# Filter stage with the edge attributes in both halves of the partitions, and register loads without bounds instructions

## The chip, the cores and the metric

The kernel runs on one core of a Trainium2 chip. The metric is the device time of one execution in microseconds (us), median of the runs. One launch computes the whole reference.

## The reference

Four graph layers on 3125 nodes with 256 features and 50000 edges sorted by destination, each followed by a residual and a layer norm:

```python
x = _layernorm(x + _L0_gnn_ref(x, edge_weight, src, dst), axis=-1)      # a product of Givens rotations
x = _layernorm(x + _L1_gnn_ref(x, ..., edge_index, edge_type_2, ...))   # three relational attention layers
x = _layernorm(x + _L2_gnn_ref(x, edge_index, edge_weight, edge_attr_50, ...))
x = _layernorm(x + _L3_gnn_ref(x, edge_index, L3_gnn_W, L3_gnn_b))      # mean over the edges by source
```

The core of L2, which the filter stage computes, is

```python
Wf = ssp(ssp(edge_attr @ m1_W + m1_b) @ m2_W + m2_b)     # ssp(x) = softplus(x) - log 2; edge_attr is (50000, 50)
msg = h1[src] * (Wf * C[:, None])
agg = jax.ops.segment_sum(msg, dst, num_segments=n_nodes)
```

In L0, the list of rotations is packed into chunks in order of the edges; in L3, `h[col]` is gathered and summed per `row`, then divided by the degree.

## The kernel before

`build` writes the stages one after the other, each in a block with a barrier of all engines at its end. Three of them are touched.

**Listing** (`layer0_list`, 0 to 222 us of the trace). The rotations are handled in five batches of 25 partition rows. `make(b)` lets VectorE write one-hot tiles (`picked`, `valued`), TensorE multiplies them (L358), 13 rows and then 12, the two halves of a batch, and `gather(b)` adds each row's block of 32 columns from PSUM into `acc` at an offset that is read from SBUF into a register (L284 to L294). VectorE's order is make(0), make(1), gather(0), make(2), gather(1), and so on to make(4), gather(3), gather(4). gather waits for the half on the semaphore `packed`. The call at L284 loads the 13 or 12 offsets of a half with one register load and then runs bounds instructions on each.

**Filter** (`filter_sum`, 4240 to 5037 us). Edges are handled in tiles of 125, four tiles (HF = 4) a quad, 106 quads. P is 125 and D is 256. Per quad:
- SyncE (`load`) waits until the hidden product of two quads before is done, reads the four tile numbers from `etile` one by one (L2515) and issues four loads of 50 x 125 attributes into `ea` (L2516). Row 50 of `ea` stays 1.0 for the bias. `load_hots` brings the one-hot matrix `sel` that sums edges into nodes (L2522).
- GpSimd gathers the source rows `gx`, one indirect DMA a tile (L2499), four quads deep; it waits for `ms_made` of the quad whose buffer it reuses.
- TensorE runs a lap of three pieces in this order: `hidden` of quad n+4 (L2545: for o in 0, 1 the product of the weights' columns o and the attributes, 51 x 128 by 51 x 500, into two PSUM banks), `sums` of quad n (L2568, or L2573 for a quad that touches more than one node tile), `filters` of quad n+3 (L2556).
- ScalarE computes the softplus parts of hidden and filters in one round (L2593 abs, L2596 exp, L2599 log); it waits for `f2_made` and `hid`.
- VectorE runs make_f2 (L2632), make_h1 (L2626), products (L2638, L2641) and the adds into `agg` (L2646: one for a quad of one node tile, else four).

The order of the work is written out by hand: each engine has its own lap of four quads, and semaphores tie them together. All matrices are fp32; the compiled program has two weight loads and two matmul instructions (passes) for each product.

**Source** (`source_mean`, 5170 to 5902 us). GpSimd gathers 424 tiles of edges (L2970) into a ring of four halves of four tiles, TensorE sums each (L2982), VectorE adds the sums into `agg` at a tile number read into a register (L3004, L3009) and makes the one-hot matrix of a later half (L2999).

## Time and profile before

| | us |
|---|---|
| median of 3 runs (lowest, highest) | 5916.76 (5911.26, 5916.9) |
| the profiled execution's own time | 5903.53 |
| its span in the trace | 5901.7 |

| engine | busy us | share |
|---|---|---|
| TensorE matmul | 4003.0 | 68% |
| TensorE weight load | 2943.7 | 50% |
| VectorE | 3007.7 | 51% |
| ScalarE | 1975.2 | 33% |
| GpSimd | 3630.7 | 62% |

The shares are means over stages with different limits. Times in the trace are counted from the start of the span. An engine's idle time is put down to what ended it; "issue" means that the engine waited for nothing that the profile shows, so its own sequencer was at work or between instructions. A matmul's recorded duration is longer than the distance to the next, since they are pipelined.

### The profile page before, as it was taken

What the parts mean: (1) busy time and instruction counts of PE and PEld (TensorE: products, weight loads), DVE (VectorE), ACT (ScalarE), POOL (GpSimd) and SP (SyncE); (2) the same over time, 40 slices, a digit from 0 to 9 for tenths busy, and PEclk for the clock granted to TensorE, in tenths of its full rate; (3) what the DMA queues carried; (4) which work ended last, traced back from release to release, by engine and by line L of the source; (5) the groups of instructions that cost most, each with busy time, mean ns of one, the idle gap of its engine ahead of it and who ended that gap; (6) DMA issues with size and microseconds to landing.
All of it is one profiled execution on the core that took longest, in us unless ns stands there. A gap on an engine that the chain in (4) does not pass through costs nothing. (4 is left out here: it accounts for less than half of the span.)

```text
span 5901.7 us, 73554 instructions
## 1 busy us (share of the span) xinstructions
PE 4003.0 (68%) x17113; PEld 2943.7 (50%) x17121; DVE 3007.7 (51%) x6900; ACT 1975.2 (33%) x4675; POOL 3630.7 (62%) x2851
## 2 busy tenths in 40 slices
PE   5599932398577778777777534445599999645553
PEld 5488831254455554355555433333376777433332
DVE  6576636621455552255555434445367777533334
ACT  0022210010466661166565112221188888200000
POOL 0144422067787754587773788885677777478884
PEclk9999975599788888888887755556799999855655
DMA  0000001333666643466663333333344444243332
GB/s 8 23 11 11 11 14 39 95 81 67 166 176 170 165 113 99 111 176 170 166 165 90 68 80 85 82 85 82 81 120 120 119 119 119 72 103 83 84 83 72
DMA packets 510802, 558.08 MB, mean 95 GB/s; under 512 B 302100, under 2 KB 394239, under 8 KB 510285
## 3 DMA queue, kind: packets, MB, share of 16 engines
q0 software_dynamic: 349600, 362.07, 25.6%
q1 hardware_dynamic: 157688, 186.99, 11.1%
q10 hardware_dynamic: 3250, 6.40, 0.4%
q14 instruction: 208, 1.70, 0.1%
q8 instruction: 56, 0.92, 0.1%
HBM read 460.15 MB, written 92.22 MB: 94 GB/s over the span
## 5 line engine op out<-in xcount | busy, mean ns | idle before, releaser
L1261 POOL DMA_INDIRECT sum_gx_sb<-scratch_xw,keep_k_row_step_sb x1272 | 1588.1, 1248 | 425.2 <-issue 358.6
L1374 PE MATMUL sum_a_ps<-sum_gx_sb,sum_sel_sb 125*125 125x258 f32 (+1 forms) x4320 | 1189.8, 438 | 454.2 <-ACT sum_gx_sb L1310 178.3
L1374 PEld LDWEIGHTS sum_a_ps<-sum_gx_sb,sum_sel_sb 125*125 125x125 f32 x4320 | 917.4, 238 | 641.5 <-issue 451.5
L1310 ACT ACTIVATE sum_gx_sb<-sum_gx_sb,sum_wt_sb 125x129 f32<-125x129 f32 x3312 | 981.8, 388 | 539.0 <-DVE sum_wt_sb L1503 539.0
L2499 POOL DMA_INDIRECT filter_gx_sb<-scratch_h,keep_k_src_step_sb x424 | 603.3, 1423 | 174.3 <-issue 97.8
L1168 POOL DMA_INDIRECT scratch_grouped<-keep_k_value_sb,keep_k_place_sb x400 | 481.1, 1203 | 250.7 <-issue 133.8
L2970 POOL DMA_INDIRECT source_gx_sb<-scratch_h,source_grouped_sb x424 | 529.5, 1249 | 140.1 <-issue 115.7
L2982 PE MATMUL source_s_ps<-source_gx_sb,source_sel_sb 125*125 125x257 f32 x848 | 376.1, 621 | 306.3 <-DMA source_gx_sb<-scratch_h,source_grouped_sb 304.8
L2982 PEld LDWEIGHTS source_s_ps<-source_gx_sb,source_sel_sb 125*125 125x125 f32 x848 | 249.0, 307 | 433.4 <-issue 170.2
L2556 PE MATMUL filter_ps<-filter_m_sb,filter_h_sb 128*125 128x256 f32 x1696 | 385.4, 380 | 1.7 <-DVE filter_h_sb L2626 1.7
L3009 DVE TENSOR_TENSOR keep_agg_sb<-source_s_ps,keep_agg_sb 125x257 f32 x424 | 181.0, 427 | 389.0 <-PE source_s_ps L2982 384.8
L533 POOL TENSOR_TENSOR turn_lm_sb<-turn_lt_sb,turn_masks_sb 128x512 f32<-128x512 f32 x23 | 29.2, 1270 | 537.7 <-DVE turn_lt_sb L467 537.7
L2556 PEld LDWEIGHTS filter_ps<-filter_m_sb,filter_h_sb 128*125 128x125 f32 x1696 | 318.8, 188 | 53.6 <-DVE filter_h_sb L2626 5.2
L1534 DVE TENSOR_TENSOR keep_agg_sb<-sum_a_ps,keep_agg_sb 125x516 f32 (+1 forms) x360 | 201.1, 559 | 147.4 <-PE sum_a_ps L1374 102.5
L1510 DVE TENSOR_TENSOR sum_sel_sb<-sum_iota_sb,keep_k_dloc_sb 125x500 f32<-125x500 f32 x324 | 219.5, 677 | 40.3 <-issue 33.0
L2545 PE MATMUL filter_ps<-filter_ea_sb,filter_m_sb 51*128 51x500 f32 x424 | 209.2, 614 | 36.4 <-DMA filter_ea_sb<-in_ea_t 36.4
L2599 ACT ACTIVATE filter_lg_sb<-filter_lg_sb,filter_half_sb 128x1000 f32<-128x1000 f32 x212 | 230.0, 1131 | 7.3
L2632 DVE TENSOR_TENSOR filter_f_sb<-filter_ps,filter_mb_sb 125x1024 f32<-125x1024 f32 x106 | 129.8, 1224 | 200.8 <-PE filter_ps L2556 200.8
L2994 ACT ACTIVATE source_root_sb<-source_root_sb 125x25 f32<-125x25 f32 x1 | 0.2, 225 | 692.7 <-DVE source_root_sb L3045 692.7
L2596 ACT ACTIVATE filter_lg_sb<-filter_lg_sb 125x1024 f32<-125x1024 f32 (+1 forms) x212 | 210.5, 1039 | 7.3
L1303 ACT ACTIVATE sum_wexp_sb<-sum_dw_sb 48x126 f32<-48x126 f32 (+1 forms) x108 | 33.1, 307 | 498.4 <-DVEq L1493 498.4
L1542 DVE SCALAR_TENSOR_TENSOR keep_agg_sb<-keep_agg_sb,sum_fac_sb,sum_a_ps 125x129 f32 x324 | 93.4, 345 | 193.4 <-PE sum_a_ps L1374 187.0
(515 smaller groups left out, 6865.6 us busy)
## 6 DMA issues: line engine op xcount, KB each, us to landing
scratch_hots<-sum_cuts_sb SPq DMA_DIRECT2D x108, 244.1 KB
filter_sel_sb<-scratch_hots SPq DMA_DIRECT2D x106, 244.1 KB
sum_gx_sb<-scratch_xw,keep_k_row_step_sb POOLq DMA_INDIRECT x1272
scratch_xw<-gate_xsb_sb SPq DMA_DIRECT2D x50, 253.9 KB
scratch_xw<-attend_xsb_sb SPq DMA_DIRECT2D x25, 507.8 KB
filter_ea_sb<-in_ea_t SPq DMA_DIRECT2D x424, 24.4 KB
filter_gx_sb<-scratch_h,keep_k_src_step_sb POOLq DMA_INDIRECT x424
source_gx_sb<-scratch_h,source_grouped_sb POOLq DMA_INDIRECT x424
```

Source lines behind the costliest of these rows:

```text
L1168: nc.gpsimd.indirect_dma_start(out=dr["grouped"], out_offset=bass.IndirectOffsetOnAxis(ap=keep["place"][:, t:t + 1], axis=0), in_=keep["va ...
L1261: nc.gpsimd.indirect_dma_start(out=gx[:, q, j, :], out_offset=None, in_=table, in_offset=bass.IndirectOffsetOnAxis(ap=keep["row_step"][:, ...
L1310: last = nc.scalar.activation(here, here, ACT.Copy, scale=wt[q][:, h, j:j + 1])
L1374: last = mm(psa[b][0:P, half, 0:BF], sel[:, 0, p, j, :], gx[:, q, at, half * BF:(half + 1) * BF], **flags)
L1510: vec.tensor_tensor(sel[:, 0, p], iota[0:P, 0:P].unsqueeze(1).broadcast_to([P, HF, P]), keep["dloc"][:, bass.ds(s * T + p * HF, HF)].unsqu ...
L2499: nc.gpsimd.indirect_dma_start(out=gx[:, n % LAP, j, :], out_offset=None, in_=dr["h2"], in_offset=bass.IndirectOffsetOnAxis(ap=keep["src_s ...
L2545: last = mm(ps1[r % 2][:, o, 0:C4], m1[0:51, 128 * o:128 * o + 128], ea[0:51, r % 2].rearrange("p j e -> p (j e)"), start=True, stop=True)
L2556: last = mm(ps2[0:P, j, :], h1[r % 2][:, b, j * P:j * P + P], m2[:, b, :], start=(b == 0), stop=(b == 1))
L2596: nc.scalar.activation(lg[:], lg[:], ACT.Exp, scale=-1.0)
L2599: nc.scalar.activation(lg[:], lg[:], ACT.Ln, scale=0.5, bias=half[0:lg.shape[0], :]).then_inc(made, 1)
L2970: nc.gpsimd.indirect_dma_start(out=gx[:, h % RING, j, :], out_offset=None, in_=dr["h3"], in_offset=bass.IndirectOffsetOnAxis(ap=grouped[:, ...
L2982: nc.tensor.matmul(pss[q % 2][0:P, j, 0:W], sel[:, q % 2, j, :], gx[:, q, j, :], start=True, stop=True).then_inc(summed, 1)
```

## The change

In the filter stage the attributes and the first weights are held twice: columns 0 to 127 of `m1` on partitions 0 to 50 and columns 128 to 255 on partitions 64 to 114, each with its copy of the attributes. SyncE issues eight loads of attributes for a quad in place of four, after one register load of four tile numbers without bounds instructions. The second product of `hidden` reads from the upper half of the partitions. Four weight loads stand at the start in place of two, and the counts of the semaphores follow. The second `If` of `sums` and of `add` becomes `Else`. In the listing and the source stage the register loads lose their bounds instructions.

```diff
@@ gather, listing stage
                     _, starts = nc.values_load_multi_w_load_instructions(
                         window[0:1, first_row:first_row + n], engines=(mybir.EngineType.DVE,), min_val=0,
-                        max_val=(NCOL - WIN) * NF)
+                        max_val=(NCOL - WIN) * NF,
+                        skip_runtime_bounds_check_because="a chunk is a rank below E over K, so a window ends within the columns")
@@ filter_sum
-    ea = mem.sb("ea", [64, 2, HF, P])
-    m1, m2, mb = mem.sb("m1", [64, D]), mem.sb("m2", [128, 2, D]), mem.sb("mb", [P, D])
+    ea = mem.sb("ea", [128, 2, HF, P])
+    m1, m2, mb = mem.sb("m1", [128, 128]), mem.sb("m2", [128, 2, D]), mem.sb("mb", [P, D])
@@ sync
-            sp.dma_start(m1[0:50, :], dr["L2_gnn_m1_W"]).then_inc(landed, 16)
-            sp.dma_start(m1[50:51, :], dr["L2_gnn_m1_b"].rearrange("(o c) -> o c", o=1)).then_inc(landed, 16)
+            for o in range(2):
+                cols = slice(128 * o, 128 * o + 128)
+                sp.dma_start(m1[64 * o:64 * o + 50, :], dr["L2_gnn_m1_W"][:, cols]).then_inc(landed, 16)
+                sp.dma_start(m1[64 * o + 50:64 * o + 51, :], dr["L2_gnn_m1_b"].rearrange("(o c) -> o c", o=1)[:, cols]).then_inc(landed, 16)
@@ load
+                    _, tiles = nc.values_load_multi_w_load_instructions(
+                        keep["etile"][0:1, bass.ds((i * LAP + r) * HF, HF)], engines=(mybir.EngineType.SP,), min_val=0,
+                        max_val=ET - 1, skip_runtime_bounds_check_because="edge tiles are made on chip within 0 and ET - 1")
                     if later(i, r, 2):
                         sp.wait_ge(hid, i * LAP + r - 1)
                     for j in range(HF):
-                        tile = sp.value_load(keep["etile"][0:1, bass.ds((i * LAP + r) * HF + j, 1)], min_val=0, max_val=ET - 1)
-                        sp.dma_start(ea[0:50, r % 2, j, :], dr["ea_t"][:, bass.ds(tile * P, P)]).then_inc(e_in[r % 2], 16)
+                        for o in range(2):
+                            sp.dma_start(ea[64 * o:64 * o + 50, r % 2, j, :], dr["ea_t"][:, bass.ds(tiles[j] * P, P)]).then_inc(e_in[r % 2], 16)
@@ hidden
-                    pe.wait_ge(e_in[r % 2], i * (LAP // 2 * 16 * HF) + (r // 2 + 1) * (16 * HF))
+                    pe.wait_ge(e_in[r % 2], i * (LAP // 2 * 32 * HF) + (r // 2 + 1) * (32 * HF))
                     for o in range(2):
-                        last = mm(ps1[r % 2][:, o, 0:C4], m1[0:51, 128 * o:128 * o + 128],
-                                  ea[0:51, r % 2].rearrange("p j e -> p (j e)"), start=True, stop=True)
+                        last = mm(ps1[r % 2][:, o, 0:C4], m1[64 * o:64 * o + 51, :],
+                                  ea[64 * o:64 * o + 51, r % 2].rearrange("p j e -> p (j e)"), start=True, stop=True)
@@ sums (TensorE), and the same in add (VectorE)
-                with pe.If(tile > NT - 1):
+                with pe.Else():
@@ add, source stage
                 _, tiles = nc.values_load_multi_w_load_instructions(
-                    keep["bucket"][0:1, bass.ds(h * HF, HF)], engines=(mybir.EngineType.DVE,), min_val=0, max_val=NT - 1)
+                    keep["bucket"][0:1, bass.ds(h * HF, HF)], engines=(mybir.EngineType.DVE,), min_val=0, max_val=NT - 1,
+                    skip_runtime_bounds_check_because="buckets are made on chip within 0 and NT - 1")
```

## Rows read from the trace of the kernel before

**Rows 1.** The page's first line.
```profile
span 5901.7 us, 73554 instructions
```

**Rows 2.** Filter stage, busy us of PE, PEld, DVE, ACT, POOL; clock, DMA share, GB/s.
```profile
4263.00:4999.00 736.00, 734.90 (x2837) 515.26 (x2837) 526.97 (x548) 619.87 (x611) 574.48 (x402) 1.00 0.46 119
```

**Rows 3.** Waits, 4260 to 5000: total us, times, longest.
```profile
DVE filter_f_sb L2632 <- PE filter_ps L2556: 195.2, 102, 5.8
ACT filter_lg_sb L2593 <- PE filter_ps L2545: 104.0, 100, 3.7
```

**Rows 4.** Timeline of TensorE's matmuls, one quad: start, us, engine, line, names, shapes.
```profile
4702.60 0.38 PE L2556 MATMUL filter_ps<-filter_m_sb,filter_h_sb 128*125 128x256 f32 x1
4702.91 0.68 PE L2545 MATMUL filter_ps<-filter_ea_sb,filter_m_sb 51*128 51x500 f32 x1
...
4703.85 1.00 PE L2545 MATMUL filter_ps<-filter_ea_sb,filter_m_sb 51*128 51x500 f32 x2
4704.27 0.58 PE L2545 MATMUL filter_ps<-filter_ea_sb,filter_m_sb 51*128 51x500 f32 x1
4704.78 0.48 PE L2568 MATMUL filter_ps<-filter_ms_sb,filter_sel_sb 125*125 125x256 f32 x1
...
4706.61 0.60 PE L2556 MATMUL filter_ps<-filter_m_sb,filter_h_sb 128*125 128x256 f32 x2
...
4710.16 0.68 PE L2545 MATMUL filter_ps<-filter_ea_sb,filter_m_sb 51*128 51x500 f32 x1
```

**Rows 5.** Timeline of TensorE's weight loads at the start of the hidden product.
```profile
4702.91 0.18 PEld L2545 LDWEIGHTS filter_ps<-filter_ea_sb,filter_m_sb 51*128 51x128 f32 x1 [0.33 <-issue]
...
4702.91 0.29 PEld L2545 LDWEIGHTS filter_ps<-filter_ea_sb,filter_m_sb 51*128 51x128 f32 x2 [0.33 <-issue]
```

**Rows 6.** Timeline of VectorE and ScalarE in the same quad.
```profile
4703.02 1.23 DVE L2632 TENSOR_TENSOR filter_f_sb<-filter_ps,filter_mb_sb 125x1024 f32<-125x1024 f32 x1 [0.38 <-PE filter_ps L2556]
4705.26 1.22 DVE L2638 SCALAR_TENSOR_TENSOR filter_f_sb<-filter_f_sb,filter_lg_sb 125x1024 f32<-125x1024 f32 x1
4704.89 1.06 ACT L2593 ACTIVATE filter_lg_sb<-filter_f_sb 125x1024 f32<-125x1024 f32 x1 [1.01 <-PE filter_ps L2545]
```

**Rows 7.** Timeline of GpSimd in the same quad, its first and fourth gather.
```profile
4700.83 1.21 POOL L2499 DMA_INDIRECT filter_gx_sb<-scratch_h,keep_k_src_step_sb  x1 [0.51 <-DVE filter_ms_sb L2641]
...
4705.38 2.19 POOL L2499 DMA_INDIRECT filter_gx_sb<-scratch_h,keep_k_src_step_sb  x1 [0.30 <-issue]
```

**Rows 8.** SyncE: one quad's attribute loads, then its instructions by line, ns min/median/max.
```profile
4700.98 4.24 SPq L2516 DMA_DIRECT2D filter_ea_sb<-in_ea_t  x4
...
L2516 SPq DMA_DIRECT2D filter_ea_sb<-in_ea_t x424: 316/317/344, 4242.6 to 5002.2; - x142
...
L2515 SPq TENSOR_LOAD <-keep_k_etile_sb x424: 426/433/631, 4241.5 to 5001.2; - x142
```

**Rows 9.** Listing stage: VectorE's instructions of L284, then timeline rows of both engines.
```profile
L284 DVEq FUSED_REGOPS  x125: 183/183/222, 69.0 to 205.7; - x125
L284 DVEq SEQ_ASSERT  x125: 23/23/41, 69.3 to 205.9; - x125
L284 DVEq TENSOR_LOAD <-listed_window_sb x10: 859/2732/2945, 67.7 to 199.5; - x10
...
54.10 42.88 PE L358 MATMUL listed_c_ps<-listed_valued_sb,listed_picked_sb 100*64 100x32 f32 x400 [14.59 <-DVE listed_valued_sb L274]
...
170.80 21.54 PE L358 MATMUL listed_c_ps<-listed_valued_sb,listed_picked_sb 100*64 100x32 f32 x200 [13.33 <-DVE listed_valued_sb L274]
...
76.80 0.18 DVE L290 TENSOR_TENSOR listed_acc_sb<-listed_acc_sb,listed_c_ps 64x32 f32 x1 [0.15 <-issue]
...
107.75 0.18 DVE L290 TENSOR_TENSOR listed_acc_sb<-listed_acc_sb,listed_c_ps 64x32 f32 x1 [6.76 <-issue]
```

**Rows 10.** Source stage: the gathers as a group, and the first add of a half.
```profile
L2970 POOL DMA_INDIRECT source_gx_sb<-scratch_h,source_grouped_sb x424 | 529.5, 1249 | 140.1 <-issue 115.7 <-PE source_s_ps L2982 13.1 <-DMA source_grouped_sb<-scratch_grouped 11.3
...
5304.98 0.43 DVE L3009 TENSOR_TENSOR keep_agg_sb<-source_s_ps,keep_agg_sb 125x257 f32 x1 [2.13 <-PE source_s_ps L2982]
```

More of the change, by code:

```diff
@@ L2533, in _ @@
             for q in range(2):
-                sp.wait_ge(e_in[q], 16 * HF * (QUADS // 2))
+                sp.wait_ge(e_in[q], 32 * HF * (QUADS // 2))
                 sp.wait_ge(hot_in[q], 16 * (QUADS // 2))
@@ L2583, in lap @@
                     filters(i, r + 3)
-            pe.wait_ge(landed, 16 * 4)
+            pe.wait_ge(landed, 16 * 6)
             laps(pe, lap)
@@ L2652, in add @@
                     one(tile, 0)
-                with dve.If(tile > NT - 1):
+                with dve.Else():
                     dve.wait_ge(summed, i * LAP + r + 1)
@@ L2680, in _ @@
             dve.nop().then_inc(added, 1)
-            dve.wait_ge(landed, 16 * 4)
+            dve.wait_ge(landed, 16 * 6)
             laps(dve, lap)
```

## The prediction, made before the changed kernel was run

> **What bounds the kernel now.** I read first the span [rows 1], then the busy table by stretch for the filter stage [rows 2], then who waits for whom there [rows 3], then single instructions of one quad [rows 4 to 8], and last the two stages in which only register loads change [rows 9, 10].
>
> In the filter stage TensorE is the bound: in 736 us it is busy for 734.9, at a granted clock of 1.00 [rows 2]. VectorE and ScalarE wait for it, 195.2 us in 102 quads and 104.0 us in 100 [rows 3]. The loop is even: the hidden product of one quad starts at 4702.91 and that of the next at 4710.16, so 7.25 us a quad: 1.87 for the hidden product, 1.83 for the sums, 3.55 for the filters [rows 4]. 736 us are 101 such quads; with start and end there are 106, and 105 of them cost or save at this rate.
>
> The listing stage is bound by VectorE's own sequencer. TensorE needs 21.5 us for a batch and then stands still until VectorE has made the next (13.33 us in the row of the last batch); before the first add of a half VectorE idles 6.76 us on "issue" [rows 9]. The source stage is bound by GpSimd: 424 gathers, 529.5 us busy and 115.7 us between them, only 13.1 us of waiting for TensorE [rows 10].
>
> **The hidden product (L2545).** Before, a quad has two fp32 products from partitions 0 to 50, each run as two passes of 500 columns, so four passes in a row. One follows the other by 0.42 us (4703.85, 4704.27) [rows 4]. The change puts the second product's weights and attributes on partitions 64 to 114 and leaves the order: A1, A2, B1, B2. A1 and A2 use the same rows of the array and must follow each other, as must B1 and B2. B1 shares neither rows nor PSUM bank with A2. If the array runs them side by side, three pass times are left: 4 x 0.42 = 1.68 becomes 1.26, a gain of 0.42 a quad, 105 x 0.42 = 44 us. No row shows two passes at once, so I bound it: nothing gained at one end (the passes stay in a row), two passes at the other. In between there is one more price, the weight load of B1. Two loads begun at 4702.91 end after 0.29 us, the first alone takes 0.18, so a load holds the next up by 0.11 [rows 5]. If B1's load starts only with A2, the gain is 0.42 - 0.11 = 0.31, or 33 us. I take the full 0.42, because in the same rows the second load goes out 0.11 us after the first, while the first pass still waits for its weights: loads don't go in step with the passes.
>
> Entering and leaving the block is not free today: the step from filters to hidden is 0.31 us where equal passes of that form take 0.22, its first pass is recorded at 0.68 against 0.58, and the step out is 0.51 against 0.42 [rows 4]. About 0.2 us at each border, twice a quad, before and after alike. The Trainium skill says in TensorEngine Tiling (Array Packing), Key Properties, that changing the tiling mode drains the engine while tiles of one mode run independently. The trace agrees as to the drain (0.2 us at each border). By that rule the step from A to B is no change of mode and adds nothing. The same page gives "up to 2x" for a contraction of at most 64 rows; its size for this program order is rival D.
>
> **What else must keep up at 6.83 us a quad.** ScalarE idles 1.01 us a quad, ended by the hidden product [rows 6], so its own round is 6.24. It starts 0.2 us after the last pass ends (4704.27 + 0.42 = 4704.69; start 4704.89). With 0.42 less that becomes 4704.47, and the other input, make_f2, is ready at 4703.02 + 1.23 = 4704.25 [rows 6]: 0.22 us to spare, so what is late next does not bite. VectorE has 195.2 / 102 = 1.9 us a quad. In the few quads that span two node tiles its four adds use that up; I charge 1 us in all. GpSimd: starts at 4700.83 and 4705.38, three steps of 1.52, then one gather of 2.19 instead of 1.21; before the first of a quad it idles 0.51, where about 0.30 lies between gathers (1.52 - 1.21) [rows 7]. The long one begins 0.12 us into VectorE's L2638 (4705.26 to 4706.48) and ends 1.09 after it, so it is held by that instruction. With a shorter quad L2638 comes earlier relative to it and the hold shrinks, so I expect no loss; kept as it is, the hold makes rival C.
>
> **Feeding the second copy.** SyncE now issues eight loads of attributes for four, but reads four registers at once. Today the four take 4.24 us, so (4.24 - 0.32) / 3 = 1.31 apart, of which 0.43 is the register load [rows 8]; the bounds work of one value is 0.18 and 0.02 where the listing stage has it [rows 9]. An issue without them costs between 0.32 (the DMA instruction alone) and 1.31 - 0.43 - 0.20 = 0.68. I take 0.5, the middle, since both ends are rows of this line. 8 x 0.5, one load of 0.6 and a hots issue of 0.5 (my estimates, from the 0.43 and the 0.5) are 5.1 us a quad (3.7 to 6.5), inside 6.83. The issues go before the hots of the same turn, which are wanted more than a quad later. On the wire a quad has 4 x 25000 bytes more, 100 KB in 7.25 us or 14 GB/s beside the 119 that give a DMA share of 0.46 [rows 2]: a share of 0.51 by bytes, 0.56 if these short rows cost double. TensorE is busy 734.9 of 736 us, so no load is late today, and each has more than a quad of lead: nothing; the two extra weight loads ahead of the first attributes cost up to 1 us once, which I leave against the passes saved in the cold start. Replacing the second test by Else takes instructions from sequencers that run ahead of a gapless TensorE: nothing. If that cover were gone, it could only gain.
>
> **Listing stage (L284).** 125 values lose one register operation of 0.183 and one check of 0.023; with gaps a value takes (6.76 - 2.94 - 0.25) / 13 = 0.275, where 2.94 is the longest register load, 13 the values of a first half, and 0.25 my estimate of what stays in front of the first add. That is 125 x 0.275 = 34.4 us, all on VectorE's path (at least the pure 0.206 x 125 = 25.8) [rows 9]. Two new waits take some back. The first batch's second half is packed at 54.10 + 21.54 = 75.6, and VectorE, which now comes to it at 77.0 [rows 9], would be there 13 x 0.275 = 3.6 earlier, so 2.2 are lost. VectorE now starts the last half's register load at 199.5, 28.7 us after TensorE starts the last batch [rows 9]; less 38 x 0.275 that is 18.2, but TensorE takes 21.5: 3.4 are lost. Sum 34.4 - 5.6 = 28.8 us, range 20 to 34.
>
> **Source stage (L3004).** The same 0.275 goes 424 times, but VectorE idles 2.13 us before the first add of a half, until TensorE releases it, against 4 x 0.275 = 1.1 us of checks [rows 10], and the stage runs at GpSimd's pace. So nothing; what hides it is the wait for the gathered rows. If the moved is_equal held more gathers, or fewer, it could be 5 us either way.
>
> **Sum.** 44 - 1 + 28.8 = 72 us. The profiled execution took 5903.5 (span 5901.7 [rows 1]), the median 5916.8, 13.2 more. 5903.5 - 72 = 5831.5, and with the 13.2: 5845. Own range: 61 us saved (weight load exposed) to 82, so 5835 to 5856.
>
> **Rivals.** B, the passes stay in a row: only the listing gain, 5917 - 29 = 5888. For it: no row shows overlap, and fp32 passes are long. B2, and the step from A to B also drains like the borders above: 105 x 0.2 = 21 given back, 5909. C, GpSimd's hold does not shrink: its round is 3 x 1.52 + 2.19 + 0.30 = 7.04 [rows 7], the gain 0.21 x 105 = 22, total 51, 5866. D, B runs beside A from the start: two passes gained, 88 - 1 + 29 = 116, 5801; against it stands the order A1, A2 ahead of B1. E, slower: SyncE becomes the bound. If each of the eight issues kept today's whole step of 1.31, a quad would take 8 x 1.31 + 0.5 = 11.0, 3.7 over today, 105 x 3.7 = 390, less 29: 6278. It decides from 7.25 us a quad on, and makes the kernel slower from 7.25 + 29 / 105 = 7.53. Against it: nearly half of the 1.31 is the work that is removed.
>
> **How the numbers follow.** Forecast 0.62, C 0.09, D 0.02, B 0.16, B2 0.05, E 0.04, and 0.02 for what I don't see. Prediction 5845. The range 5832 to 5892 takes in the forecast, C and B. A measurement can tell 0.2% (12 us) from no change. Faster by more: forecast, B, C, D and half of the rest, 0.90. Within: B2, 0.05. Slower: E and the other half, 0.05.
>
> **What would show it.** Right: quads 6.83 us apart, B1 starting with A2 or up to 0.11 after it; the clock in the stage still 1.00; listing over 29 us earlier, with TensorE, not "issue", ahead of the last half's first add; the source stage of equal length. Wrong: hidden passes still 0.42 apart in a row (B), the idle of GpSimd between quads at 0.30 (C), TensorE waiting for DMA of the attributes (E), a granted clock that falls.

## The result, and the profile after

The changed kernel takes 5810.08 us (median of 4 runs, 5807.12 to 5817.56) against 5914.88 for the kernel before beside it (4 runs, 5911.26 to 5916.9): a ratio of 0.9825, 95% interval 0.9808 to 0.9842. That is 104.8 us less, where the prediction had 72, and the time lies below the predicted range (5832 to 5892). The profiled execution took 5807.12. In two more groups of runs the changed kernel took 5801.22 and 5811.7 beside 5910.19 and 5914.55: 109.0 and 102.9 less, ratios of 0.9822 and 0.9821. One execution of one variant below, that with both products in the lower half, took 7481.15 us at a mean granted clock of 0.605, where all others had 0.77 to 0.80, and is left out of its numbers.

The filter stage by stretch, changed kernel (us, busy time and instructions of PE, PEld, DVE, ACT and POOL; then the granted clock, the DMA share and GB/s), with the line that answers to [rows 2]:

```profile
span 5805.0 us, 71815 instructions
4300.00:4900.00 600.00, 596.36 (x2588) 435.28 (x2588) 482.22 (x505) 562.37 (x556) 462.36 (x370) 1.00 0.58 149
```

TensorE is still the bound, busy 596.4 of 600 us, at a granted clock of 1.00, though it now has 3.6 us of gaps. In the same 600 us it starts 2588 matmul passes (2321 before), and ScalarE is busy for 562 us, near its own limit. One quad on TensorE, in the places of [rows 4] (start, us, engine, line, count of passes):

```profile
4600.90 0.38 PE L2562 MATMUL filter_ps<-filter_m_sb,filter_h_sb 128*125 128x256 f32 x1
4601.21 0.69 PE L2551 MATMUL filter_ps<-filter_ea_sb,filter_m_sb 51*128 51x500 f32 x2
...
4601.21 1.11 PE L2551 MATMUL filter_ps<-filter_ea_sb,filter_m_sb 51*128 51x500 f32 x4
4602.25 1.99 PE L2574 MATMUL filter_ps<-filter_ms_sb,filter_sel_sb 125*125 125x256 f32 x8
4604.08 3.62 PE L2562 MATMUL filter_ps<-filter_m_sb,filter_h_sb 128*125 128x256 f32 x16
4607.63 0.69 PE L2551 MATMUL filter_ps<-filter_ea_sb,filter_m_sb 51*128 51x500 f32 x2
```

Two hidden passes start at 4601.21 and last 0.69 us together, as long as one alone in [rows 4]; all four last 1.11. The distance from the first of them to the first of the sums is 1.04 us, where it was 1.87 in [rows 4]. The sums still take 1.83 and the filters 3.55. So the quad went from 7.25 to 6.42 us (4601.21 to 4607.63): 0.83 less, two pass times. The borders are what they were: 0.31 us from the last filter pass to the block.

Waits of the stage in the same stretch (total us, times, longest), for [rows 3]:

```profile
DVE filter_f_sb L2638 <- PE filter_ps L2562: 71.9, 56, 1.3
...
DVE filter_f_sb L2638 <- issue: 28.2, 36, 1.3
ACT filter_lg_sb L2599 <- issue: 16.4, 60, 1.3
ACT filter_lg_sb L2599 <- DVE filter_f_sb L2638: 8.8, 19, 1.3
```

VectorE still waits for TensorE in 56 of the 92 quads or so, for 1.3 us where it waited for 1.9; in most of the others the same idle time is put down to "issue". ScalarE no longer stands in the list as waiting for the hidden product (104.0 us before); what is left are 16.4 and 8.8 us. Single rows of ScalarE, VectorE, GpSimd and SyncE's queue, for [rows 6], [rows 7] and [rows 8] (L2644 here is L2638 of the kernel before):

```profile
4602.65 1.06 ACT L2599 ACTIVATE filter_lg_sb<-filter_f_sb 125x1024 f32<-125x1024 f32 x1 [0.18 <-issue]
```
```profile
4603.56 1.22 DVE L2644 SCALAR_TENSOR_TENSOR filter_f_sb<-filter_f_sb,filter_lg_sb 125x1024 f32<-125x1024 f32 x1
```
```profile
4604.60 1.27 POOL L2500 DMA_INDIRECT filter_gx_sb<-scratch_h,keep_k_src_step_sb  x1 [0.30 <-issue]
4606.38 1.22 POOL L2500 DMA_INDIRECT filter_gx_sb<-scratch_h,keep_k_src_step_sb  x1 [0.51 <-DVE filter_ms_sb L2647]
```
```profile
4604.42 0.26 SPq L2528 DMA_DIRECT2D filter_sel_sb<-scratch_hots  x1
4605.47 2.40 SPq L2522 DMA_DIRECT2D filter_ea_sb<-in_ea_t  x6
```

ScalarE idles 0.18 us ahead of its round (1.01 before). GpSimd's fourth gather takes 1.27 us where it took 2.19. It still begins while VectorE runs L2644, but 1.04 us into it, with 0.18 us of it left. SyncE issues six of the eight loads in 2.40 us, 0.4 us each.

A few quads are slower, those in which VectorE adds to four node tiles (start, us; the idle time ahead in brackets):

```profile
4488.99 0.42 DVE L2652 TENSOR_TENSOR keep_agg_sb<-filter_ps,keep_agg_sb 125x256 f32 x1
...
4490.76 0.42 DVE L2652 TENSOR_TENSOR keep_agg_sb<-filter_ps,keep_agg_sb 125x256 f32 x1 [0.17 <-issue]
4491.82 1.22 DVE L2638 TENSOR_TENSOR filter_f_sb<-filter_ps,filter_mb_sb 125x1024 f32<-125x1024 f32 x1 [0.64 <-issue]
```

The four adds take 2.2 us in place of 0.42, and make_f2 of the next quad starts behind them without waiting for TensorE. From the starts of L2551, 14 quads take 6.76 to 7.31 us; together they take some 7.3 us more than 14 quads of 6.42.

The listing stage, for [rows 9]: VectorE's first adds of the two halves that now wait, and TensorE's last batch and the transposes behind it:

```profile
78.45 0.18 DVE L291 TENSOR_TENSOR listed_acc_sb<-listed_acc_sb,listed_c_ps 64x32 f32 x1 [5.23 <-issue]
...
176.18 0.18 DVE L291 TENSOR_TENSOR listed_acc_sb<-listed_acc_sb,listed_c_ps 64x32 f32 x1 [6.39 <-issue]
```
```profile
151.73 21.54 PE L359 MATMUL listed_c_ps<-listed_valued_sb,listed_picked_sb 100*64 100x32 f32 x200 [6.38 <-DVE listed_valued_sb L274]
184.75 1.95 PE L368 MATMUL listed_t_ps<-listed_ident_sb,listed_rows_of_sb 128*100 128x128 f32 x8 [11.48 <-DVEq L310]
```

and the same transposes in the kernel before:

```profile
214.62 1.95 PE L367 MATMUL listed_t_ps<-listed_ident_sb,listed_rows_of_sb 128*100 128x128 f32 x8 [22.28 <-DVEq L309]
```

They come 29.9 us earlier. In the source stage the gathers run from 5087.2 to 5743.1 us, 655.9 us, against 657.1 (5182.1 to 5839.2) in the kernel before.

### The profile page after: what moved, and what is told of

The parts are those of the page before. It is cut to its first block and busy times, and to the rows that moved or that the text cites. A ratio compares the mean times of both kernels' runs of the same rounds, so it can differ in the third digit from the quotient of the medians.

```text
span 5805.0 us, 71815 instructions
## 1 busy us (share of the span) xinstructions
PE 3909.2 (67%) x17120; PEld 2896.3 (50%) x17121; DVE 3008.5 (52%) x6900; ACT 1974.3 (34%) x4675; POOL 3564.8 (61%) x2851
## 5 line engine op out<-in xcount | busy, mean ns | idle before, releaser
L2500 POOL DMA_INDIRECT filter_gx_sb<-scratch_h,keep_k_src_step_sb x424 | 529.4, 1249 | 168.9 <-issue 99.1
L2638 DVE TENSOR_TENSOR filter_f_sb<-filter_ps,filter_mb_sb 125x1024 f32<-125x1024 f32 x106 | 129.8, 1224 | 123.3 <-PE filter_ps L2562 91.1
L2574 PE MATMUL filter_ps<-filter_ms_sb,filter_sel_sb 125*125 125x256 f32 x720 | 180.6, 394 | 6.2 <-issue 6.2
```

Source lines behind the costliest of these rows:

```text
L2500: nc.gpsimd.indirect_dma_start(out=gx[:, n % LAP, j, :], out_offset=None, in_=dr["h2"], in_offset=bass.IndirectOffsetOnAxis(ap=keep["src_s ...
```

## The experiments

**Do the parts add up, and does the rest of the kernel stand still?** The first three went together: the changed kernel again, the listing stage's part alone, and the filter stage's part alone.

> The changed kernel, unaltered, once more. The stage boundaries of the two profiles said that the filter stage gained 81.5 us and the listing stage 29.9, 111.4 together, while the profiled time fell by 96.4: some 16 us came back in stages between them that the change doesn't touch. If that is variation from execution to execution, the new profile moves the start of the filter stage by more than 5 us against the first profile of the changed kernel (4226 us) while its length stays at 713.8 within 1. If it is an effect of the change, the filter stage begins at 4226 within 2 again. The time in both: 5810 within 8.

Measured: 5801.22 us (5792.71 to 5814.9), before beside it 5910.19 (5905.61 to 5913.55, 8 runs), ratio 0.9822 [0.9804, 0.984]. That is 0.8 us outside the "within 8". In its profile the filter stage begins at 4219.5 us, 6.7 earlier than in the first profile (4226.2), and lasts 714.6 against 714.8 us, as expected for variation (both lengths to the end of the stage's last instruction, hence 714.8 and not 713.8).

```diff
-                        max_val=(NCOL - WIN) * NF)
+                        max_val=(NCOL - WIN) * NF,
+                        skip_runtime_bounds_check_because="a chunk is a rank below E over K, so a window ends within the columns")
```

> The kernel before with the listing stage's offsets loaded without bounds instructions, nothing else. The stage should end at 186.7 us in place of 216.6. Theory 1 (the gain of the listing stage stays): 5915 less 30, 5885 within 4. Theory 2 (some of it is given back in the attention stages, because they start at another time): 5895 to 5902.

Measured: 5880.4 us, ratio 0.9955 [0.9938, 0.9971], so 29.8 less than the kernel before beside it: theory 1 by the difference, though the time itself is 0.6 us outside the "within 4". Its transposes start at 184.74 us, as in the changed kernel.

```diff
-                        max_val=(NCOL - WIN) * NF,
-                        skip_runtime_bounds_check_because="a chunk is a rank below E over K, so a window ends within the columns")
+                        max_val=(NCOL - WIN) * NF)
...
-                    keep["bucket"][0:1, bass.ds(h * HF, HF)], engines=(mybir.EngineType.DVE,), min_val=0, max_val=NT - 1,
-                    skip_runtime_bounds_check_because="buckets are made on chip within 0 and NT - 1")
+                    keep["bucket"][0:1, bass.ds(h * HF, HF)], engines=(mybir.EngineType.DVE,), min_val=0, max_val=NT - 1)
```

> The changed kernel with the bounds instructions back in the listing and the source stage, so the filter stage's part alone. Theory 1 (parts add): 5915 less 81.5, 5833 within 4, with the filter stage some 714 us long. Theory 2 (the change of the listing stage cost some 16 us further on): the stages between listing and filter are as long as before, and the time is 5833 as well, but the changed kernel less this one is then 16 us short of the listing stage's 30: 5810 against 5833 is 23, against 30 by theory 1.

Measured: 5825.3 us, ratio 0.9856 [0.984, 0.9873], 84.9 less, somewhat more than expected. Its filter stage lasts 715.3 us, within 1 of the changed kernel's. 29.8 and 84.9 make 114.7 where both together gave 109.0 beside the same runs, and the changed kernel is 24.1 us below this one, nearer to theory 2's 23 than to theory 1's 30. The changed kernel's four runs spread over 22 us, so the times don't decide between the two; the profiles say more. For the stages between, the attention stages' gathers (count; shortest, middle and longest in ns; first and last start), first the kernel before, then the changed kernel, the listing part alone and the filter part alone:

```profile
L1261 POOL DMA_INDIRECT sum_gx_sb<-scratch_xw,keep_k_row_step_sb x1272: 1205/1211/2376, 1490.7 to 4030.4; - x182
```
```profile
L1262 POOL DMA_INDIRECT sum_gx_sb<-scratch_xw,keep_k_row_step_sb x1272: 1207/1214/2377, 1468.8 to 4014.4; - x182
```
```profile
L1262 POOL DMA_INDIRECT sum_gx_sb<-scratch_xw,keep_k_row_step_sb x1272: 1205/1212/2205, 1467.5 to 4006.8; - x182
```
```profile
L1261 POOL DMA_INDIRECT sum_gx_sb<-scratch_xw,keep_k_row_step_sb x1272: 1205/1212/1868, 1491.4 to 4036.6; - x182
```

They last 2539.7, 2545.6, 2539.3 and 2545.2 us. The filter part alone is longer there by 5.5 us although nothing before the filter stage differs from the kernel before; the changed kernel lasted 2545.3 and 2551.4 us in two further profiles, and a version that holds the whole change (the early offsets, below) 2539.5. From the transposes of the listing stage to the first instruction of the filter stage, the three profiles with the old listing take 4025.0 (the kernel before), 4033.4 and 4037.9 us, the eleven with the new one 4032.1 to 4050.0. So the 16 us or so that seemed to be given back are for the most part variation between executions, and the profiled execution of the kernel before was the quickest of all. That a few us come back because of the change isn't excluded.

**Is all of the filter stage's gain the overlap?** Both products read the lower half again; the eight loads and the new register load stay:

```diff
-                        last = mm(ps1[r % 2][:, o, 0:C4], m1[64 * o:64 * o + 51, :],
-                                  ea[64 * o:64 * o + 51, r % 2].rearrange("p j e -> p (j e)"), start=True, stop=True)
+                        last = mm(ps1[r % 2][:, o, 0:C4], m1[0:51, 128 * o:128 * o + 128],
+                                  ea[0:51, r % 2].rearrange("p j e -> p (j e)"), start=True, stop=True)
```

> The changed kernel with both hidden products read from the lower half of the partitions; the attributes are still loaded into both halves, eight loads a quad, and the whole of the first weights lies in both halves (four weight loads of twice the columns). Theory 1 (all of the filter stage's gain is two passes running beside two others): a quad takes 7.25 us again, the stage 795 us, the time 5810 + 105 x 0.83 less 6 for mixed quads whose adds are hidden again = 5890 to 5897. Theory 2 (a part of the gain is SyncE's: one register load in place of four, attributes there earlier): a quad below 7.2 us, the time below 5885. Theory 3 (eight loads a quad cost something that the overlap covers): above 5900.

Measured: 5883.64 us (4 runs, 5881.48 to 5886.46), ratio 0.9957 [0.9941, 0.9973], 26.6 below the kernel before. One quad on TensorE:

```profile
4605.06 1.94 PE L2550 MATMUL filter_ps<-filter_ea_sb,filter_m_sb 51*128 51x500 f32 x4
4606.93 1.99 PE L2573 MATMUL filter_ps<-filter_ms_sb,filter_sel_sb 125*125 125x256 f32 x8
...
4612.31 1.94 PE L2550 MATMUL filter_ps<-filter_ea_sb,filter_m_sb 51*128 51x500 f32 x4
```

The block takes 1.87 us and a quad 7.25 again. Against the changed kernel in the same group the overlap is worth 5883.6 - 5801.2 = 82.4 us, and feeding both halves costs nothing that can be seen. The length of the quad decides for theory 1. The time came out 6 to 13 us below what it gave, since the changed kernel of this group lay 9 us below the 5810 that the sum started from.

**What does the second product cost while it runs beside the first?** The upper product is left out (ScalarE reads zeros in its place):

```diff
-                    for o in range(2):
-                        last = mm(ps1[r % 2][:, o, 0:C4], m1[64 * o:64 * o + 51, :],
-                                  ea[64 * o:64 * o + 51, r % 2].rearrange("p j e -> p (j e)"), start=True, stop=True)
+                    last = mm(ps1[r % 2][:, 0, 0:C4], m1[0:51, :],
+                              ea[0:51, r % 2].rearrange("p j e -> p (j e)"), start=True, stop=True)
```

> The changed kernel without the hidden product of the upper half: only the one of the lower half is made, so half of the hidden values are wrong; everything else stands as it is, the eight loads too. Theory 1 (the upper product runs wholly beside the lower one and costs nothing): 6.42 us a quad still, the filter stage and the time as in the changed kernel, 5800 to 5812. Theory 2 (the two products share something, so that two at once are dearer than one): a quad below 6.42.

Measured: 5806.79 us, ratio 0.9818 [0.9801, 0.9834]. Its quad:

```profile
4599.70 3.62 PE L2561 MATMUL filter_ps<-filter_m_sb,filter_h_sb 128*125 128x256 f32 x16
4603.25 1.10 PE L2550 MATMUL filter_ps<-filter_ea_sb,filter_m_sb 51*128 51x500 f32 x2
4604.28 1.99 PE L2573 MATMUL filter_ps<-filter_ms_sb,filter_sel_sb 125*125 125x256 f32 x8
4606.11 2.11 PE L2561 MATMUL filter_ps<-filter_m_sb,filter_h_sb 128*125 128x256 f32 x9
```

1.03 us for two passes alone, 1.04 for all four in the changed kernel; 6.41 us a quad. That is theory 1: the second product is free to 0.01 us.

**Does the order within the block matter?** Each product in two of 250 columns, in the order lower, lower, upper, upper:

```diff
                     for o in range(2):
-                        last = mm(ps1[r % 2][:, o, 0:C4], m1[64 * o:64 * o + 51, :],
-                                  ea[64 * o:64 * o + 51, r % 2].rearrange("p j e -> p (j e)"), start=True, stop=True)
+                        for c in range(2):
+                            last = mm(ps1[r % 2][:, o, 250 * c:250 * c + 250], m1[64 * o:64 * o + 51, :],
+                                      ea[64 * o:64 * o + 51, r % 2, 2 * c:2 * c + 2].rearrange("p j e -> p (j e)"), start=True, stop=True)
```

> The changed kernel with each hidden product cut into two of 250 columns, in the order lower, lower, upper, upper (four instructions, eight passes of about 0.21 us). Theory 1 (TensorE starts a pass of the other half of the partitions as soon as it is next in the program, not earlier, and the two passes of one fp32 product are not a bar to its neighbour): only the second and the third product run beside each other, so 1.26 us of hidden passes a quad where the changed kernel has 0.84: 6.84 a quad, 5810 + 105 x 0.42 = 5854 within 6. Theory 2 (the half whose turn it isn't is passed over freely, so the order of the products doesn't matter): 6.42 a quad, 5810. Theory 3 (strict order of passes, only the last of one half beside the first of the other): 1.47 us of hidden passes, 7.05 a quad, 5876.

Measured: 5805.72 us beside 5903.53 for the kernel before (7 runs), ratio 0.9828 [0.9812, 0.9845].

```profile
4604.07 0.49 PE L2552 MATMUL filter_ps<-filter_ea_sb,filter_m_sb 51*128 51x250 f32 x2
...
4604.07 1.12 PE L2552 MATMUL filter_ps<-filter_ea_sb,filter_m_sb 51*128 51x250 f32 x8
4605.13 1.99 PE L2580 MATMUL filter_ps<-filter_ms_sb,filter_sel_sb 125*125 125x256 f32 x8
```

Two of the eight short passes start at 4604.07, and the sums follow 1.06 us later. A quad takes 6.43 us, where theories 1 and 3 wanted 6.84 and 7.05. The rows don't say which half a pass belongs to, but passes of one half can't share a start (with both products in one half they followed one another for 1.87 us). So the first pass of the upper half starts beside the first of the lower, though the kernel's text has another whole product of the lower half ahead of it. That is theory 2 as far as the kernel's text goes. Whether TensorE passes over the half whose turn it isn't, or the compiled program already holds the passes in another order, isn't shown: the trace has no list of the program's order. One number speaks for TensorE. The second start of a block comes 7 ns after the first in the changed kernel and 13 ns here, in the median of 106 blocks each, as if two passes of the lower half had been taken in first there and four here.

**And across products of another form?** The order lower, sums, upper, filters:

```diff
-                    for o in range(2):
+                    for o in (0,):
...
+            def hidden_upper(i, r):
+                if runs(i, r):
+                    last = mm(ps1[r % 2][:, 1, 0:C4], m1[64:115, :],
+                              ea[64:115, r % 2].rearrange("p j e -> p (j e)"), start=True, stop=True)
...
                         sums(i, r, tiles[r])
+                    hidden_upper(i, r + 4)
                     filters(i, r + 3)
```

> The changed kernel with the order of TensorE changed: the lower hidden product, then the sums (125 rows), then the upper hidden product, then the filters. Theory 1 (TensorE starts the other half's product early only if nothing of over 64 rows stands between them, and each change between products of 51 rows and of 125 costs about 0.2 us, 0.39 for a pair): 6.42 + 0.84 + 0.39 = 7.65 us a quad, 5810 + 105 x 1.23 less some 5 for the mixed quads, 5925 to 5940. Theory 2 (the upper product is pulled forward beside the lower one wherever it stands): 6.42 to 6.8 a quad. Theory 3 (the overlap goes, but the borders cost nothing here): 7.26, 5890 to 5895.

Measured: 5923.26 us beside 5911.73 for the kernel before (13 runs), ratio 1.0021 [1.0011, 1.003]: slower than the kernel before by 11.5 us, and 116.5 slower than the kernel without the upper product in the same group.

```profile
4606.09 1.10 PE L2551 MATMUL filter_ps<-filter_ea_sb,filter_m_sb 51*128 51x500 f32 x2
4607.12 1.99 PE L2579 MATMUL filter_ps<-filter_ms_sb,filter_sel_sb 125*125 125x256 f32 x8
4609.05 1.10 PE L2556 MATMUL filter_ps<-filter_ea_sb,filter_m_sb 51*128 51x500 f32 x2
...
4613.73 1.10 PE L2551 MATMUL filter_ps<-filter_ea_sb,filter_m_sb 51*128 51x500 f32 x2
```

4606.09 to 4613.73 is 7.64 us a quad, theory 1's 7.65: the upper product doesn't start before the sums, and two more borders are paid. The time is just below the 5925 expected. What holds it back isn't shown: the sums have 125 rows, but a wait for three semaphores stands in front of them too, and the run puts both in between.

**What do the borders cost?** In the kernel before, the hidden products get 128 rows, those from 51 on with weights of zero (and SyncE's first wait moves ahead of the weight loads):

```diff
-    ea = mem.sb("ea", [64, 2, HF, P])
-    m1, m2, mb = mem.sb("m1", [64, D]), mem.sb("m2", [128, 2, D]), mem.sb("mb", [P, D])
+    ea = mem.sb("ea", [128, 2, HF, P])
+    m1, m2, mb = mem.sb("m1", [128, D]), mem.sb("m2", [128, 2, D]), mem.sb("mb", [P, D])
...
-                        last = mm(ps1[r % 2][:, o, 0:C4], m1[0:51, 128 * o:128 * o + 128],
-                                  ea[0:51, r % 2].rearrange("p j e -> p (j e)"), start=True, stop=True)
+                        last = mm(ps1[r % 2][:, o, 0:C4], m1[0:128, 128 * o:128 * o + 128],
+                                  ea[0:128, r % 2].rearrange("p j e -> p (j e)"), start=True, stop=True)
...
+            vec.memset(m1[:], 0.0)
```

> The kernel before with the hidden products read from all 128 partitions, the weights of rows 51 to 127 set to zero: the same four passes of 500 columns in a row, but with as many rows as their neighbours have. Theory 1 (the 0.2 us or so that TensorE stands at each change from products of over 64 rows to products of 51 and back goes away): a quad takes 6.85 to 7.05 in place of 7.25, 5894 to 5873. Theory 2 (those 0.2 us belong to something else, the waits for a semaphore or the fp32 weights): 7.25, 5915.

Measured: 5866.09 us, ratio 0.993 [0.9913, 0.9946], 37.4 less.

```profile
4599.64 3.62 PE L2556 MATMUL filter_ps<-filter_m_sb,filter_h_sb 128*125 128x256 f32 x16
4603.10 1.84 PE L2545 MATMUL filter_ps<-filter_ea_sb,filter_m_sb 128*128 128x500 f32 x4
4604.77 1.89 PE L2568 MATMUL filter_ps<-filter_ms_sb,filter_sel_sb 125*125 125x256 f32 x8
4606.50 1.68 PE L2556 MATMUL filter_ps<-filter_m_sb,filter_h_sb 128*125 128x256 f32 x7
```

The block takes 1.67 us, four passes of 0.42, in place of 1.87, sums and filters 0.19 less together, and the quad 6.86 (4599.64 to 4606.50) in place of 7.25: 0.39 us a quad for the two borders. That is theory 1, at its better end.

**What makes 14 quads slow?**

```diff
-                    for j in range(HF):
-                        one(tiles[j], j)
+                    one(tiles[0], 0)
```

> The changed kernel in which VectorE adds only the first of the four node tiles for a quad that touches more than one, so three adds to agg are left out in each of these quads. In the changed kernel 14 quads take 6.76 to 7.31 us in place of 6.42, 7.5 us over in all. Theory 1 (VectorE's four adds are the cause, since TensorE's lap has become shorter): these quads fall to 6.42 and the time to 5802 or 5803. Theory 2 (the four separate sums on TensorE, or loading their tile numbers, is the cause): they stay within 0.1 and the time at 5808 to 5810.

Measured: 5794.47 us (5781.26 to 5803.05), ratio 0.9804 [0.9785, 0.9823]. The time lies below the 5802 to 5803 of theory 1, with the runs 22 us apart, and alone doesn't settle it; the profile does: after the start all 101 quads take 6.41 or 6.42 us. The gathers of the changed kernel and of this one:

```profile
L2500 POOL DMA_INDIRECT filter_gx_sb<-scratch_h,keep_k_src_step_sb x424: 1207/1214/1991, 4227.0 to 4917.8; - x142
```
```profile
L2500 POOL DMA_INDIRECT filter_gx_sb<-scratch_h,keep_k_src_step_sb x424: 1207/1211/1367, 4230.8 to 4915.4; - x142
```

690.8 against 684.6 us, and the longest gather falls from 1.99 to 1.37 us. So theory 1 holds.

**What is late next in the filter stage?** Two of four sums are left out:

```diff
-                    for j in range(HF):
-                        last = mm(ps3[0:P, 0, :], sel[:, r % 2, j, :], ms[r % 2][:, j, :], start=(j == 0), stop=(j == HF - 1))
+                    for j in range(2):
+                        last = mm(ps3[0:P, 0, :], sel[:, r % 2, j, :], ms[r % 2][:, j, :], start=(j == 0), stop=(j == 1))
```

> The changed kernel with two of the four sums products left out in each quad of one node tile (the sums are of half the edges), which takes four passes of about 0.23 us, 0.9 us, from TensorE: what is late next in the filter stage. Theory 1 (ScalarE is next, since it has 0.18 us to spare ahead of each round of 6.24 us): a quad takes 6.24 us, 0.18 less, and the time is 16 to 20 us below the changed kernel's. Theory 2 (TensorE is the bound by itself with nothing behind it): 5.5 us a quad, some 85 us less. Theory 3 (SyncE with eight loads a quad, or GpSimd with its gathers, is next): a length other than 6.24, and these queues show no waits.

Measured: 5816.33 us (5806.98 to 5823.87), ratio 0.9832 [0.9812, 0.9851], beside 5811.7 for the changed kernel: nothing gained. Of 105 quads 57 take 6.14 us, which is ScalarE's round when it waits for nothing. (The 6.24 taken from [rows 6] is 0.1 too long, since an operation that waits for nothing starts some 0.1 us before the recorded end of the one ahead: after the row at 4602.65, recorded to 4603.71, the next starts at 4603.62.) But 31 take 6.17 to 6.87 and 16 take 7.0 to 9.6, the four-tile quads among them. VectorE's idle time ahead of make_f2 in 4250 to 4900 us, then the filter passes of the longest quad but one and those of another quad, and the granted clock (the last column but two) around the first of them:

```profile
DVE filter_f_sb L2638 <- issue: 61.2, 63, 2.7
```
```profile
4600.00 5.40 PE L2562 MATMUL filter_ps<-filter_m_sb,filter_h_sb 128*125 128x256 f32 x16 [2.03 <-issue]
...
4817.06 3.72 PE L2562 MATMUL filter_ps<-filter_m_sb,filter_h_sb 128*125 128x256 f32 x16 [2.70 <-DVE filter_h_sb L2632]
```
```profile
4596.00:4600.00 4.00, 1.97 (x8) 0.77 (x6) 2.76 (x4) 1.98 (x3) 3.31 (x3) 1.00 0.61 160
...
4601.00:4604.00 3.00, 3.00 (x8) 2.33 (x8) 1.64 (x3) 2.87 (x4) 1.21 (x1) 0.50 0.53 133
```

TensorE, no longer the bound, stood idle for 2.03 us up to 4600.00. From 0.8 us after it had started again the granted clock was 0.50, the 1.2 GHz of its two levels, in place of 1.00, for some 3 us: 16 filter passes took 5.4 us where they take 3.6. Between 4260 and 4900 us this happened in two places, here and at 4341.4, around the end of 2.15 us of idle time. Yet after 2.67 us of idle time (up to 4718.49) and after 2.70 (the second row) the clock stayed at 1.00, so the length of the idle time alone doesn't tell when it falls. The lower clock is a price of a shorter share of TensorE in the loop, here some 2 us each time. Theory 2 is out. Theory 1 is right that ScalarE sets the floor, but the stage doesn't stay on it: four-tile quads, VectorE's stalls ahead of make_f2 and the lower clock take it back. The cause of VectorE's stalls isn't shown. The changed kernel has such quads too, in its third profile two, of 7.82 and 8.53 us.

> The changed kernel unaltered, as the yardstick on the same chip for the two others of this group: 5801 to 5810, quads of 6.42 us. By the theory that the stages which the change doesn't touch vary from one execution to the next, its profile has the filter stage begin anywhere from 4218 to 4230 us, its length within 1 us of 713.8.

Measured: 5811.7 us (5799.24 to 5813.44), ratio 0.9821 [0.9805, 0.9837]. The stage began where expected, at 4225.7, but lasted 7 us longer than in the first profile (722.2 against 714.8), not within 1: two of its quads hold such a stall, the longer of them this one, for which the profile names nothing of this kernel that it waited for:

```profile
4656.84 1.22 DVE L2638 TENSOR_TENSOR filter_f_sb<-filter_ps,filter_mb_sb 125x1024 f32<-125x1024 f32 x1 [3.62 <-remote]
```

**A version that beats both.** The listing stage leaves VectorE idle some 3 us ahead of each half for its register loads. They are moved ahead of make's drain:

```diff
+            def offsets(b):
+                found = []
+                for h in range(2):
+                    first_row, n = b * BATCH + h * SPLIT, half_rows[h]
+                    _, starts = nc.values_load_multi_w_load_instructions(window[0:1, first_row:first_row + n], ...)
+                    found.append(starts)
+                return found
...
                         [T100, NTB, WIN, NF]), ALU.mult).then_inc(dve_picked, 1)
+                found = offsets(b - 1) if b else None
                 dve.drain()
+                return found
...
-                make(b)
-                gather(b - 1)
-            gather(NBATCH - 1)
+                gather(b - 1, make(b))
+            gather(NBATCH - 1, offsets(NBATCH - 1))
```

> The changed kernel, in whose listing stage the register loads of a batch's 25 offsets stand between the last large operation of make and its drain, in place of behind the wait of each half (L284). In the changed kernel VectorE stands about 3 us ahead of each half's first add, twice a batch. Theory 1 (VectorE's sequencer runs ahead of its operations, so the loads are hidden behind the 5.6 us of L274): a batch takes some 22 us in place of 28, limited by TensorE's 21.5 us; the stage ends at 162 to 167 us in place of 187, the time falls by 20 to 25. Theory 2 (register loads wait until the operations before them are done): the 6 us a batch only move ahead of the drain, the stage ends at 187 within 3 and the time is that of the changed kernel.

Measured: 5790.38 us (5788.55 to 5800.89) beside 5811.7 for the changed kernel and 5914.55 for the kernel before (9 runs), ratio to the latter 0.9796 [0.9781, 0.9812].

```profile
93.25 0.18 DVE L299 TENSOR_TENSOR listed_acc_sb<-listed_acc_sb,listed_c_ps 64x32 f32 x1 [0.30 <-issue]
```
```profile
94.78 66.00 PE L366 MATMUL listed_c_ps<-listed_valued_sb,listed_picked_sb 100*64 100x32 f32 x617
169.49 1.95 PE L375 MATMUL listed_t_ps<-listed_ident_sb,listed_rows_of_sb 128*100 128x128 f32 x8 [8.71 <-DVEq L317]
```

The first add now comes 0.30 us after the operation ahead of it; TensorE runs without a gap, ends at 160.8 instead of 173.3 us, and the transposes start at 169.49, 15.3 us before the changed kernel's 184.75. The loads are hidden, which is theory 1. The stage saves 15.3 us and not 20 to 25: TensorE keeps to its 21.5 us a batch, as expected, but 8.71 us of idle time for VectorE's last work still stand between its end and the transposes, which the expected end of the stage left no room for. The medians differ by 21.3 us; what is over 15.3 is within the spread of the runs.

## Why the prediction was wrong in size

- **Bound and mechanism: right.** TensorE set the pace before and after, and the gain in the filter stage is hidden passes running side by side: without the overlap 82.4 of the 109.0 us go.
- **The step that failed** is "Three pass times are left", which rested on the order A1, A2, B1, B2. Two are left. The block went from 1.87 to 1.04 us, so the term is 0.83 and not 0.42 a quad, 105 x 0.83 = 87 us in place of 44. Rival D had this and was given a chance of 0.02. The prediction ruled it out by the order of the program, but no row showed what TensorE does with that order when two row halves are in use, as the kernel before never used the other one. The run with the order lower, lower, upper, upper shows that within the block the order of the kernel's text doesn't bind.
- **Order of the passes.** The Trainium skill, in TensorE: Matmul & The Clock Gate, Part 3 (Packing small matmuls), says that products in different tiles of the array run at the same time, and the trace agrees (two passes in 0.69 us). The same part, under What overlaps and what doesn't, says that matmuls start and end strictly in program order. Here a pass of the upper half starts beside the first of the lower with a whole product between them in the kernel's text (4604.07), so for these fp32 products the measurement speaks against it, unless the compiled program had another order, which no trace shows.
- **The range stopped too early at its fast end.** "Nothing gained" and "two passes" were both named as ends, but the range of the sum stopped at one pass; the end of 88 us belonged in it. Its 82 us saved follow from no term either: 44 - 1 + 34.4 is 77.
- **Borders: right.** "About 0.2 us at each border, twice a quad": 0.39 a quad, by the run with full rows. Going from lower to upper half costs no border, or 1.04 could not equal 1.03.
- **Mixed quads: mis-sized.** Charged at 1 us, they cost 6 (gathers with and without the three adds, 690.8 against 684.6) to 7 (the 14 quads): VectorE's 1.9 us of waiting shrank to 1.3 with the quad, while three more adds take 1.8 and 0.64 of branch and semaphores stands behind them. The step used the waiting of the kernel before, not what is left of it at 6.83 or 6.42.
- **Listing: right.** 28.8 forecast, 29.9 measured, with both new waits where they were named: ahead of the second half of the first batch (5.23 us idle) and of the last half (6.39). The sign named for it was wrong: both rows say "issue" and not TensorE, because the register loads stand between the wait and the first add.
- **ScalarE: right in kind.** 0.22 us to spare was forecast with one pass gained; with two, ScalarE idles 0.18 and is no longer released by the hidden product in the list of waits. It now nearly sets the pace; VectorE still has 1.3 us a quad, but not in the quads with four adds.
- **GpSimd (rival C): right to be out.** The hold shrinks with the quad, as said. Before, the gather began with 1.10 us of VectorE's instruction left and ended 1.09 after it; now it begins with 0.18 left and again ends 1.09 after it (4605.87 against 4604.78), so 2.19 us became 1.27. Of the 424 gathers 93 took more than 1.9 us before and 10 do now. In the run with sums between, whose quad is 7.64, none starts within that instruction and all take at most 1.24 us. (The sum in C is 7.05, not 7.04; nothing hangs on it.)
- **SyncE (rival E): right to be out.** The loads are issued 0.4 us apart (0.5 forecast). The DMA share is 0.58, over both estimates (0.51 by bytes, 0.56 with short rows at double cost), since a quad is shorter too: 0.58 x 6.42 / 7.25 is 0.51, the estimate by bytes. In the steady stretch TensorE still waits for no DMA.
- **Source stage: right.** 1.2 us shorter.
- **From profile to median.** The profiles differ by 96.4 us: 87 - 7 + 30 + 1 = 111 less about 16 of variation in the stages between. The profile before lay 13.2 us below its median and the one after 3.0, so 10 of the 16 us are this one quick execution, and the medians differ by 104.8. Adding the 13.2 to the profile's time was right, and no part of the miss.

## What to carry to other kernels

A product of 51 rows left room for a second one beside it. With a copy of the operands in the other half of the partitions the second was free here (1.04 against 1.03 us), in both orders that were tried. With a product of 125 rows in between the overlap is lost, and each pair of borders costs 0.39 us. Where nothing can run beside it, padding a short product to full rows with zero weights removes the borders; that gave 0.39 us a quad for no work. Where a forecast rests on what the hardware does in a state that no row shows, let the range reach to both ends. Read a slack at the pace that the change will bring, not at today's. Register loads between a long operation and its drain were hidden (0.30 us of idle time in place of 3.17).

## What the runs showed of the hardware that I had not expected

- Fp32 passes on the other half of the rows start ahead of their turn in the kernel's text: two of the eight passes start at 4604.07, with a whole product between them in the text. Whether TensorE or the compiled program puts them there is open.
- Four passes on two halves take 1.04 us, two passes on one half 1.03.
- Padding 51 rows to 128 makes the block faster, 1.67 against 1.87 us, and the quad 0.39 us shorter.
- In the run with two sums left out, the granted clock fell to 0.50 for some 3 us around the ends of 2.03 and 2.15 us of idle time of TensorE, and did not after 2.67 and 2.70. The 16 passes of the first place took 5.4 us in place of 3.6.
- A gather on GpSimd that starts within VectorE's product of two SBUF tiles ends 1.08 to 1.10 us after it, whether 1.10 or 0.18 us of it were left: so all 97 such gathers of the kernel before and all 83 of the changed one.
- With ScalarE near its limit, single quads of 7 to 9.6 us appear in some profiles, in which VectorE stands for up to 3.62 us. What it waits for is open.
- The same gathers of the attention stages take from 2539 to 2554 us in one execution or another of the fourteen, so two single profiles of this kernel can't be compared to better than some 15 us over these stages.
